# Comparisons for one-hots merged across tiles, buckets and units in the building stage of a graph network kernel

## The chip, the cores and the metric

The program runs on one core of a Trainium2 chip. The metric is the device time of one execution in microseconds, lower is better. The median of three executions stands for a kernel.

## The reference

The kernel computes two graph network layers over 12,500 nodes of 64 features and 412,500 edges `(src, dst)`, sorted by `dst`. Layer 0 is a hypergraph convolution, used twice, whose sums run over the edges in both directions; layer 1 makes a message for each edge from both its ends and a weight, sums it at the row, and feeds a node network.

```python
def _hypergraph_conv(x, node_idx, edge_idx, D_inv, B_inv, W, b):
    xt = x @ W
    e = B_inv[:, None] * segment_sum(xt[node_idx], edge_idx, num_segments=NUM_HYPEREDGES)
    out = D_inv[:, None] * segment_sum(e[edge_idx], node_idx, num_segments=NUM_NODES)
    return out + b
...
h = maximum(_layernorm(x), 0.0)
x = x + _L0_gnn_ref(h, edge_index, ...)
h = maximum(_layernorm(x), 0.0)
x = x + _L1_gnn_ref(h, src, dst, edge_weight1, ...)
```

The sums over edges of layer 0 are done as matrix products: the kernel first builds the adjacency as a matrix of small counts, block by block (how many edges go from node m to node d), and then multiplies with it. The stage that builds it is called the building here; the change lies in it alone.

## The kernel before

**Chunks, tiles, groups.** The building goes through the edges in 49 chunks (`NCH`), each for 256 destination nodes. A chunk holds 70 tiles (`TC`) of 128 edges, in 14 groups (`NGR`) of five (`GT`). 102 buckets (`KEYS`) take the edges of a chunk by the block of 128 nodes of their source (98 of them, and four for the diagonal). A loop iteration holds two turns; a turn does the 14 groups of one chunk and, beside them, the 50 units of the chunk before it. In the groups 2 to 13 stand 42 units, three or four to a group, and the last eight (`LATE`) come in groups 0 and 1 of the next turn.

**A group, over five engines.** POOL writes the one-hots `OH` of five tiles, 128 x 102 bf16 each (`onehots`, L662; it runs up to a turn ahead). PE turns them into running counts per bucket in the PSUM bank `R` (`ranks`, L777 to L785). ACT copies the last tile's counts to `cb` for the next group (`count`, L910) and widens `OH` to fp32 (`widen`, L916). DVE takes for each edge its rank, that is its slot in its bucket, into `rk` (`ranks`, L1018 to L1020), and writes one-hots of the slot (`places`): for the first three tiles (`AT`) as bf16 in `LB` (L1032), which ACT then multiplies with the two payloads `pl` into `LH` (`scaled`, L926, six copies a group); for the other two DVE makes the multiplied one-hot `LH` at once (L1038). PE multiplies `OHf` and `LH` into the bank `S` (`buckets`, L799), one group later, between the second and the third unit of a group. The width of a one-hot grows from 16 to 88 slots over the first seven groups, and again over the last seven.

**A unit.** The filled buckets are transposed (`turned`), and DVE copies them to `SBk`, `SBe` and `SBd` (`sorted_`). Unit 0 is the diagonal; each of the units 1 to 49 takes two buckets, an even one and an odd one. For it DVE compares a column of sources and one of destinations with a row of numbers (`unit`, in pairs of units). For the even bucket the source one-hot is in `OA`, for the odd one in `OB` with the value 256; both destination one-hots are in `OD` (L1089 to L1097). PE sums the two products into 256 columns of one of four PSUM banks, `bank(u)`, so that a sum is even count + 256 x odd count (`counts`, L825 and L826). ACT copies it to `RB` as int16, which is two bytes, each the fp8 code of a small count, and sums the row into `gs` (`keep`, L965):

```python
e.matmul(b[:, 0:256], lhsT=even, rhs=OD[k % PAIRS][:, y, :, 0], start=True, stop=False)
ins = e.matmul(b[:, 0:256], lhsT=odd, rhs=OD[k % PAIRS][:, y, :, 1], start=False, stop=True)
...
e.activation(RB[n % NSLOT][:, k, :].bitcast(i16), bank(u)[:, 0:256], ACT.Copy,
             accum_out=gs[:, u:u + 1]).then_inc(a_u, 1)
```

Three units later PE multiplies `RB` with the node features (`sums`, L841, four products). SP stores `RB`, in seven pieces of seven units, also transposed. Twice a turn DVE takes the row sums `gs` apart into their two bytes and keeps the greatest (`counted`, L1138 to L1145).

**What sets the order.** Each engine runs its list in the order in which the functions `step` and `turn` write it; semaphores hold it back. `past` and `wait_ge` are such waits. Rings of buffers bound the distance: two of `R`, `LB`, `LH` and `OHf`, five (`PAIRS`) of `OA`, `OB` and `OD`, four banks `PS`, four pieces of `RB`.

The stages after the building read the stored blocks, multiply with them, and do layer 1. Their lines are numbered from about 1215 on.

## Time and profile before

| | us |
|---|---|
| median of three executions | 8857.22 |
| lowest, highest | 8846.52, 8869.20 |
| the profiled execution | 8864.02 |
| its span, first to last instruction | 8862.3 |
| the building in it, from the page's slices | about 200 to 3340 |

The profile is of one execution. Its time and its span differ by 1.7 us, which lie around the instructions. Busy times of an engine count the time in which at least one of its instructions runs; consecutive instructions of DVE and ACT overlap by some 0.1 us, so durations of single ones add up to more than the busy time, and the distance from start to start tells what one costs in a row. A timeline row merges equal neighbours (x3) and gives the start of the first and the time to the end of the last.

### The profile page before, as it was taken

How to read it: one execution, taken by the hardware profiler on the slowest of the kernel's cores; microseconds unless marked ns; L12 is line 12 of the kernel's file. 1: busy time of each engine (PE TensorE's matmuls, PEld its weight loads, DVE VectorE, ACT ScalarE, POOL GpSimd, SP SyncE). 2: the span in 40 equal slices, each digit the busy share in tenths (PEclk: the TensorE clock that was granted, in tenths of full speed). 3: DMA queues.
4: the chain of work that ended last, by engine and by line, in shares of the span. 5: the costliest groups of instructions: out<-in, count | busy, mean ns of one | idle time of the engine just before them, and what ended most of it. 6: DMA issues, size and time to landing. Idle time of an engine off the chain costs nothing. (4 is left out here: it accounts for less than half of the span.)

```text
span 8862.3 us, 258190 instructions
## 1 busy us (share of the span) xinstructions
PE 7877.5 (89%) x80997; PEld 7191.2 (81%) x80997; DVE 7406.3 (84%) x20481; ACT 5157.5 (58%) x14322; POOL 2812.5 (32%) x4182
## 2 busy tenths in 40 slices
PE   2989998999989988999888899869999999999997
PEld 2777777777777778999788888759998999999995
DVE  7999999999999995777688888548888888888884
ACT  3777777777777770000577788425555555555553
POOL 4977778777777750000000000001111111111110
PEclk9999999999999999999799999759999999999998
DMA  2767667766676677666699999643333333333333
GB/s 71 158 152 157 154 153 157 155 155 153 156 156 153 156 159 199 190 191 170 148 223 222 214 245 245 139 142 109 104 106 106 103 106 106 105 104 105 107 104 74
DMA packets 1523049, 1310.03 MB, mean 148 GB/s; under 512 B 797344, under 2 KB 1337364, under 8 KB 1521212
## 3 DMA queue, kind: packets, MB, share of 16 engines
q1 hardware_dynamic: 1506126, 1269.86, 58.6%
q0 software_dynamic: 14112, 26.84, 1.2%
q8 instruction: 593, 9.72, 0.4%
q14 instruction: 378, 3.10, 0.1%
q10 hardware_dynamic: 1840, 0.53, 0.0%
HBM read 777.89 MB, written 361.62 MB: 129 GB/s over the span
## 5 line engine op out<-in xcount | busy, mean ns | idle before, releaser
L662 POOL TENSOR_SCALAR OH<-iot,kd 128x102 bf16<-128x102 bf16 x3440 | 2285.3, 683 | 3.5 <-PE S L799 3.5
L2257 POOL DMA_INDIRECT Qx<-tab_q,tidx x294 | 320.9, 1091 | 4904.5 <-DVE skt L2291 2584.5
L1478 PE MATMUL wp<-AF,XS 128*128 128x256 f32 x9604 | 1196.3, 283 | 167.6 <-issue 123.4
L841 PE MATMUL HP<-T3a,RB 128*128 128x193 bf16 x9604 | 1209.2, 249 | 124.3 <-ACT RB L965 124.3
L1478 PEld LDWEIGHTS wp<-AF,XS 128*128 128x128 f32 x9604 | 1148.5, 191 | 198.4 <-issue 198.3
L1504 ACT ACTIVATE AF<-RG 128x1536 fp32r<-128x1536 uint8 x686 | 1022.9, 1491 | 332.6 <-PE wp L1478 226.0
L965 ACT ACTIVATE RB<-PS 128x256 int16<-128x256 f32 x2401 | 895.6, 379 | 520.2 <-PE PS L826 479.2
L2278 ACT ACTIVATE Z<-Zb 128x512 f32<-128x512 f32 x882 | 556.1, 630 | 994.3 <-DVE Zb L2335 948.8
L841 PEld LDWEIGHTS HP<-T3a,RB 128*128 128x128 fp8e4 x9604 | 858.8, 98 | 249.1 <-issue 160.8
L926 ACT ACTIVATE LH<-LB,pl 128x64 f32<-128x64 bf16 (+8 forms) x4116 | 1008.4, 330 | 0.0
L2335 DVE TENSOR_TENSOR Zb<-p,eb2s 128x512 f32<-128x512 f32 x882 | 609.3, 691 | 450.1 <-PE p L2228 276.9
L2228 PEld LDWEIGHTS p<-eW2s,Y 128*128 128x128 f32 x7056 | 940.2, 194 | 31.8 <-issue 7.3
L2228 PE MATMUL p<-eW2s,Y 128*128 128x128 f32 x7056 | 947.7, 278 | 4.0 <-issue 3.8
L1558 DVE CAST AF<-RG 128x2048 fp32r<-128x2048 uint8 x686 | 812.3, 1222 | 148.7 <-PE wp L1478 55.0
L1097 DVE TENSOR_TENSOR OD<-iot,SBd 128x512 bf16<-128x512 bf16 x2401 | 932.6, 427 | 0.0
L799 PE MATMUL S<-LH,OHf 128*102 128x144 f32 (+9 forms) x6860 | 863.2, 274 | 14.4 <-ACT LH L926 11.8
L1343 PE MATMUL hp<-ACC,RG 128*128 128x193 bf16 x9604 | 822.1, 247 | 4.0 <-DMA RG<-adjT 4.0
L1343 PEld LDWEIGHTS hp<-ACC,RG 128*128 128x128 fp8e4 x9604 | 814.8, 98 | 7.9 <-issue 4.2
L799 PEld LDWEIGHTS S<-LH,OHf 128*102 128x102 f32 x6860 | 770.5, 172 | 42.4 <-issue 32.9
L825 PE MATMUL PS<-OD,OA 128*128 128x256 bf16 x2401 | 668.5, 279 | 150.3 <-DVE OD L1097 142.5
L2271 ACT ACTIVATE Y<-pT,eb1s 128x512 f32<-128x512 f32 x882 | 592.1, 671 | 221.1 <-remote 136.6
L2240 PE MATMUL pA<-Zp,Os 128*128 128x256 f32 x3528 | 649.7, 307 | 25.2 <-DVE Zp L2343 25.0
(344 smaller groups left out, 15460.4 us busy)
## 6 DMA issues: line engine op xcount, KB each, us to landing
RG<-adjT SPq DMA_DIRECT2D x1372, 224.0 KB, 6.6
sdb<-bk SPq DMA_DIRECT2D x245, 768.0 KB
adj<-RB SPq DMA_DIRECT2D x343, 448.0 KB, 2.8
adjT<-RT SPq DMA_DIRECT2D x686, 224.0 KB, 3.8
...
WR<-wk SPq DMA_DIRECT2D x882, 9.0 KB
...
```

Source lines behind the costliest of these rows:

```text
L662: ins = e.tensor_scalar(OH[:, g * GT + k, :], iot1[:, 0:KEYS], kd[:, g * GT + k:g * GT + k + 1], None, ALU.is_equal)
L799: ins = e.matmul(slots_to(g, w), lhsT=OHf[g % 2][:, k, :], rhs=LH[g % 2][:, k, :, 0:w], start=False, stop=True, skip_group_check=True)
L825: e.matmul(b[:, 0:256], lhsT=even, rhs=OD[k % PAIRS][:, y, :, 0], start=True, stop=False)
L841: ins = e.matmul(HP[:, h * W3:(h + 1) * W3], lhsT=pair[:, x_, h * P:(h + 1) * P], rhs=T3a[:, 2 * (u - 1) + x_, :], start=False, stop=True, ...
L926: ins = e.activation(LH[g % 2][:, k, c, 0:w], LB[g % 2][:, k, 0:w], ACT.Copy, scale=pl[:, c, t:t + 1])
L965: e.activation(RB[n % NSLOT][:, k, :].bitcast(i16), bank(u)[:, 0:256], ACT.Copy, accum_out=gs[:, u:u + 1]).then_inc(a_u, 1)
L1097: ins = e.tensor_tensor(OD[k % PAIRS][:, y, :, :], iot2[:, :, :], SBd[:, b + 2 * y:b + 2 * y + 2].unsqueeze(1).to_broadcast([P, 256, 2]), ...
L1343: ins = e.matmul(ps[b][:, h * W:(h + 1) * W], lhsT=piece(n, k_, h), rhs=tin3[:, n * 2 * PIECE + k_, 0:W], start=False, stop=True, skip_gro ...
L1478: ins = e.matmul(ps[b][:, 0:256], lhsT=XS[:, n * PB + m, :, :].rearrange("p c f -> p (c f)"), rhs=AF[:, (b + n) % 3, m, :], start=n == 0 a ...
L1504: e.activation(floats((b + n) % 3, VB, PB), counts(n, VB, PB), ACT.Copy).then_inc(h_ca, 1)
L1558: e.tensor_copy(floats((b + n) % 3, 0, VB), counts(n, 0, VB)).then_inc(h_cd, 1)
L2228: ins = e.matmul(p2[g % 2][:, t * P:(t + 1) * P], lhsT=Y[g % 2][:, t * P:(t + 1) * P], rhs=nW["eW2s"][:, :], start=True, stop=True)
```

## The change

Four things change, all in the building.

- **Slot one-hots.** DVE writes the bf16 one-hots `LB` of all five tiles with one comparison, as wide as the widest of the five, with fp32 inputs (`places`). ACT multiplies two tiles of a group (`AT` is 2) and DVE the other three, in one instruction, after the units of the group (`scaled`).
- **Source and destination one-hots.** One comparison writes `OA` for the four buckets of a pair of units, and one writes `OD` for both units. `OB` is gone.
- **Counts.** The products of the even and the odd bucket go to separate halves of the bank, 256 columns each, and ACT copies 512 values to bytes, reading the two halves in turn.
- **The check of row sums** needs no taking apart: one maximum instead of five instructions.

```diff
@@ -21,7 +21,7 @@
-AT = 3
+AT = 2
@@ -509,11 +507,11 @@
-OA = [sbt(p1, f"OA{n}", [P, 2 * P], bf16) for n in range(PAIRS)]
-OB = [sbt(p1, f"OB{n}", [P, 2, P], bf16) for n in range(PAIRS)]
+OA = [sbt(p1, f"OA{n}", [P, 4 * P], bf16) for n in range(PAIRS)]
 OD = [sbt(p1, f"OD{n}", [P, 2, 256, 2], bf16) for n in range(PAIRS)]
-SBe = sbt(p1, "SBe", [P, NCH], bf16)
+iot4 = sbt(p1, "iot4", [P, P, 4], bf16)
+SBs = sbt(p1, "SBs", [P, BLK], bf16)
@@ -591,9 +588,16 @@
-def by_rank(g, up, down, w):
-    return up[:, 0:w] if g < HG else down[:, P - w:P]
+def used(t):
+    w, g = wide_at(t), t // GT
+    a = 0 if g < HG else wide_at(g * GT + GT - 1) - w
+    return slice(a, a + w)
+def by_rank(g, n, w):
+    v = iofo[:, 0:w] if g < HG else iofr[:, P - w:P]
+    return v.unsqueeze(1).to_broadcast([P, n, w])
@@ -796,7 +800,7 @@
-                ins = e.matmul(slots_to(g, w), lhsT=OHf[g % 2][:, k, :], rhs=LH[g % 2][:, k, :, 0:w],
+                ins = e.matmul(slots_to(g, w), lhsT=OHf[g % 2][:, k, :], rhs=LH[g % 2][:, k, :, used(g * GT + k)],
@@ -820,10 +824,10 @@
-                even = OA[k % PAIRS][:, 0:n * P].rearrange("p (m y) -> p m y", y=n)[:, :, y]
-                odd = OB[k % PAIRS][:, y, :]
-                e.matmul(b[:, 0:256], lhsT=even, rhs=OD[k % PAIRS][:, y, :, 0], start=True, stop=False)
-                ins = e.matmul(b[:, 0:256], lhsT=odd, rhs=OD[k % PAIRS][:, y, :, 1], start=False, stop=True)
+                at = OA[k % PAIRS][:, 0:2 * n * P].rearrange("p (m y) -> p m y", y=2 * n)
+                e.matmul(b[:, 0:256], lhsT=at[:, :, 2 * y], rhs=OD[k % PAIRS][:, y, :, 0], start=True, stop=True)
+                ins = e.matmul(b[:, 256:512], lhsT=at[:, :, 2 * y + 1], rhs=OD[k % PAIRS][:, y, :, 1],
+                               start=False, stop=True, skip_group_check=True)
@@ -921,9 +925,9 @@
             past(e, p_s, i * NGR + (g - 1))
             for k in range(AT):
                 t = g * GT + k
-                w = wide_at(t)
+                w = used(t)
                 for c in range(2):
-                    ins = e.activation(LH[g % 2][:, k, c, 0:w], LB[g % 2][:, k, 0:w], ACT.Copy, scale=pl[:, c, t:t + 1])
+                    ins = e.activation(LH[g % 2][:, k, c, w], LB[g % 2][:, k, w], ACT.Copy, scale=pl[:, c, t:t + 1])
             ins.then_inc(a_lh, 1)
         def record(c):
@@ -962,8 +966,8 @@
-            e.activation(RB[n % NSLOT][:, k, :].bitcast(i16), bank(u)[:, 0:256], ACT.Copy,
-                         accum_out=gs[:, u:u + 1]).then_inc(a_u, 1)
+            e.activation(RB[n % NSLOT][:, k, :].bitcast(u8).rearrange("p (n x) -> p n x", x=2),
+                         bank(u)[:, :].rearrange("p (x n) -> p n x", x=2), ACT.Copy, accum_out=gs[:, u:u + 1]).then_inc(a_u, 1)
@@ -1018,27 +1022,25 @@
             e.tensor_reduce(rk[:, t:t + GM], R[g % 2][:, 0:GM * KEYS].rearrange("p (t k) -> p t k", k=KEYS), AX, ALU.max)
             t += GM
             e.tensor_tensor_reduce(out=rj[:, :], in0=R[g % 2][:, GM * KEYS:GT * KEYS], in1=OH[:, t, :],
-                                   scale=1.0, scalar=0.0, op0=ALU.mult, op1=ALU.add, accum_out=rk[:, t:t + 1]).then_inc(v_rk, 1)
-        def places(i, g, pl):
+                                   scale=1.0, scalar=float(OWN - 1), op0=ALU.mult, op1=ALU.add, accum_out=rk[:, t:t + 1]).then_inc(v_rk, 1)
+        def places(i, g):
             e.wait_ge(v_rk, i * NGR + (g + 1))
             if g == NGR - 1:
                 e.tensor_tensor(mxr[:, :], mxr[:, :], rk[:, :], ALU.max).then_inc(v_mx, 1)
             past(e, p_s, i * NGR + (g - 1))
             past(e, a_lh, i * NGR + (g - 1))
-            for k in range(AT):
-                t = g * GT + k
-                w = wide_at(t)
-                ins = e.tensor_scalar(LB[g % 2][:, k, 0:w], by_rank(g, iot1, iotr, w), float(OWN - 1), rk[:, t:t + 1], ALU.add, ALU.is_equal)
-            ins.then_inc(v_lb, 1)
-            for k in range(AT, GT):
-                t = g * GT + k
-                w = wide_at(t)
-                ranked = by_rank(g, iofo, iofr, w) if k < GM else by_rank(g, iot1, iotr, w)
-                ins = e.scalar_tensor_tensor(LH[g % 2][:, k, :, 0:w], ranked.unsqueeze(1).to_broadcast([P, 2, w]),
-                                             rk[:, t:t + 1], pl[:, :, t:t + 1].to_broadcast([P, 2, w]),
-                                             ALU.is_equal, ALU.mult)
-            ins.then_inc(v_lh, 1)
+            t, w = g * GT, wide_at(g * GT + GT - 1)
+            e.tensor_tensor(LB[g % 2][:, :, 0:w], by_rank(g, GT, w), rk[:, t:t + GT].unsqueeze(2).to_broadcast([P, GT, w]),
+                            ALU.is_equal).then_inc(v_lb, 1)
+        def scaled(i, g, pl):
+            e.wait_ge(v_lb, i * NGR + (g + 1))
+            n, t, w = GT - AT, g * GT, wide_at(g * GT + GT - 1)
+            e.tensor_tensor(LH[g % 2][:, AT:GT, :, 0:w], LB[g % 2][:, AT:GT, 0:w].unsqueeze(2).to_broadcast([P, n, 2, w]),
+                            pl[:, :, t + AT:t + GT].rearrange("p c t -> p t c").unsqueeze(3).to_broadcast([P, n, 2, w]),
+                            ALU.mult).then_inc(v_lh, 1)
         def filled(i):
@@ -1058,8 +1060,8 @@
-            e.tensor_copy(SBk[:, :], S[:, TR:TR + 2 * KEYS])
-            e.tensor_copy(SBe[:, :], S[:, TR:TR + BLK].rearrange("p (n x) -> p n x", x=2)[:, :, 0])
+            e.tensor_copy(SBk[:, :], S[:, TR + KEYS + BLK:TR + 2 * KEYS])
+            e.tensor_copy(SBs[:, :], S[:, TR:TR + BLK])
@@ -1078,25 +1080,18 @@
             if u == 0:
                 past(e, p_u, c * NU + (1 - NU))
                 for q in range(4):
-                    b = KEYS + BLK + q
-                    ins = e.tensor_scalar(OZ[:, q, :], iot1[:, :], SBk[:, b:b + 1], None, ALU.is_equal)
+                    ins = e.tensor_scalar(OZ[:, q, :], iot1[:, :], SBk[:, q:q + 1], None, ALU.is_equal)
                 ins.then_inc(v_un, 1)
             elif u % 2:
                 k = (u - 1) // 2
                 past(e, p_u, c * NU + (2 * k - 7 if k != 4 else 0))
-                for y in range(2 if u < NU - 1 else 1):
-                    b = 2 * (u + y - 1) + 1
-                    e.tensor_scalar(OB[k % PAIRS][:, y, :], iot1[:, 0:P], SBk[:, b:b + 1], 256.0, ALU.is_equal, ALU.mult)
+                n = 2 if u < NU - 1 else 1
                 b = 2 * (u - 1)
-                if u < NU - 1:
-                    e.tensor_tensor(OA[k % PAIRS][:, :].rearrange("p (m y) -> p m y", y=2), iot2[:, 0:P, :],
-                                    SBe[:, u - 1:u + 1].unsqueeze(1).to_broadcast([P, P, 2]), ALU.is_equal)
-                else:
-                    e.tensor_scalar(OA[k % PAIRS][:, 0:P], iot1[:, 0:P], SBk[:, b:b + 1], None, ALU.is_equal)
-                for y in range(2 if u < NU - 1 else 1):
-                    ins = e.tensor_tensor(OD[k % PAIRS][:, y, :, :], iot2[:, :, :],
-                                          SBd[:, b + 2 * y:b + 2 * y + 2].unsqueeze(1).to_broadcast([P, 256, 2]), ALU.is_equal)
-                ins.then_inc(v_un, 1)
+                e.tensor_tensor(OA[k % PAIRS][:, 0:2 * n * P].rearrange("p (m y) -> p m y", y=2 * n), (iot4 if n == 2 else iot2)[:, 0:P, :],
+                                SBs[:, b:b + 2 * n].unsqueeze(1).to_broadcast([P, P, 2 * n]), ALU.is_equal)
+                e.tensor_tensor(OD[k % PAIRS][:, 0:n, :, :], iot2[:, :, :].unsqueeze(1).to_broadcast([P, n, 256, 2]),
+                                SBd[:, b:b + 2 * n].rearrange("p (y x) -> p y x", x=2).unsqueeze(2).to_broadcast([P, n, 256, 2]),
+                                ALU.is_equal).then_inc(v_un, 1)
         def finish(c, n):
@@ -1132,17 +1127,9 @@
         def counted(c, h):
             a, b = (1, NU // 2) if h == 0 else (NU // 2, NU)
-            seen = c * 10 + (h * 5 + 1)
             e.wait_ge(a_u, c * NU + b)
-            e.wait_ge(v_gs, seen)
-            e.tensor_copy(gi[:, a:b], gs[:, a:b]).then_inc(v_gs, 1)
-            e.wait_ge(v_gs, seen + 1)
-            e.tensor_scalar(gl[:, 0, a:b], gi[:, a:b], 255, None, ALU.bitwise_and).then_inc(v_gs, 1)
-            e.tensor_scalar(gl[:, 1, a:b], gi[:, a:b], 8, None, ALU.arith_shift_right).then_inc(v_gs, 1)
-            e.wait_ge(v_gs, seen + 3)
-            e.tensor_tensor(mg[:, a:b], mg[:, a:b], gl[:, 0, a:b], ALU.max).then_inc(v_gs, 1)
-            e.wait_ge(v_gs, seen + 4)
-            e.tensor_tensor(mg[:, a:b], mg[:, a:b], gl[:, 1, a:b], ALU.max).then_inc(v_gs, 1)
+            e.wait_ge(v_gs, c * 2 + (h + 1))
+            e.tensor_tensor(mg[:, a:b], mg[:, a:b], gs[:, a:b], ALU.max).then_inc(v_gs, 1)
         def step(i, u, before):
             unit(i, u)
@@ -1171,11 +1158,13 @@
                 if rank:
                     if g == 0:
                         e.wait_ge(v_ld, i + 1)
-                    places(i, g, pl[b])
+                    places(i, g)
                 if unit_ and g == 2:
                     parts(i - 1)
                 for u in us[early:]:
                     step(k, u, before)
+                if rank:
+                    scaled(i, g, pl[b])
         e.wait_ge(c_init, 4)
         turn(0, 0, True, False, False, False)
```

DVE, near the end of a turn (group 12: a pair of units, then the places of the group, then the next pair). `c_pu`, `c_ps`, `c_alh`, `c_rk` and `c_vlb` are semaphores that PE's units, PE's buckets, ACT's copies, the ranks and the places raise. Before:

```order
L1089 TENSOR_SCALAR OB<-iot,SBk 128x128 [waits c_pu]
L1089 TENSOR_SCALAR OB<-iot,SBk 128x128
L1092 TENSOR_TENSOR OA<-iot,SBe 128x256
L1097 TENSOR_TENSOR OD<-iot,SBd 128x512 x2
L1032 TENSOR_SCALAR LB<-iotr,rk 128x72 [waits c_alh,c_ps,c_rk]
L1032 TENSOR_SCALAR LB<-iotr,rk 128x72 x2
L1038 SCALAR_TENSOR_TENSOR LH<-iofr,rk,pl 128x2x72
L1038 SCALAR_TENSOR_TENSOR LH<-iotr,rk,pl 128x2x80
```

and after:

```order
L1090 TENSOR_TENSOR OA<-iot,SBs 128x512 [waits c_pu]
L1092 TENSOR_TENSOR OD<-iot,SBd 128x1024
L1034 TENSOR_TENSOR LB<-iofr,rk 128x5x80 [waits c_alh,c_ps,c_rk]
L1041 TENSOR_TENSOR LH<-LB,pl 128x6x80 [waits c_vlb]
L129 REGISTER_ALU
L1090 TENSOR_TENSOR OA<-iot,SBs 128x512 [waits c_pu]
L1092 TENSOR_TENSOR OD<-iot,SBd 128x1024
```

Five instructions of the pair have become two, and five of the places have become two, the second of which waits for the first.

ACT, a group with four units (`c_pr`, `c_oh` and `c_pu` are raised by PE's ranks, POOL and PE's units). Before:

```order
L910 ACTIVATE cb<-R 128x102 [waits c_pr]
L916 ACTIVATE OHf<-OH 128x510 [waits c_ps,c_oh]
L948 REGISTER_ALU
L965 ACTIVATE RB,rows_of<-PS 128x256 [waits c_pu]
L948 REGISTER_ALU
L965 ACTIVATE RB,rows_of<-PS 128x256 [waits c_pu]
L948 REGISTER_ALU
L965 ACTIVATE RB,rows_of<-PS 128x256 [waits c_pu]
L948 REGISTER_ALU
L965 ACTIVATE RB,rows_of<-PS 128x256 [waits c_pu]
L926 ACTIVATE LH<-LB,pl 128x64 [waits c_ps,c_vlb]
L926 ACTIVATE LH<-LB,pl 128x64 x5
```

and after:

```order
L914 ACTIVATE cb<-R 128x102 [waits c_pr]
L920 ACTIVATE OHf<-OH 128x510 [waits c_ps,c_oh]
L952 REGISTER_ALU
L969 ACTIVATE RB,rows_of<-PS 128x512 [waits c_pu]
L952 REGISTER_ALU
L969 ACTIVATE RB,rows_of<-PS 128x512 [waits c_pu]
L952 REGISTER_ALU
L969 ACTIVATE RB,rows_of<-PS 128x512 [waits c_pu]
L952 REGISTER_ALU
L969 ACTIVATE RB,rows_of<-PS 128x512 [waits c_pu]
L930 ACTIVATE LH<-LB,pl 128x64 [waits c_ps,c_vlb]
L930 ACTIVATE LH<-LB,pl 128x64 x3
```

The order is the same; each unit's copy is twice as long in elements, and two of the six scaled copies are gone.

## Rows read from the trace of the kernel before

**Rows 1.** The profile page, its first section: busy time, share of the span, instructions.
```profile
PE 7877.5 (89%) x80997; PEld 7191.2 (81%) x80997; DVE 7406.3 (84%) x20481; ACT 5157.5 (58%) x14322; POOL 2812.5 (32%) x4182
```

**Rows 2.** Busy time of each engine in a stretch of the building: window, PE, PEld, DVE, ACT, POOL, PEclk, DMA share, GB/s.
```profile
1500.00:2500.00 1000.00, 906.61 (x8423) 762.74 (x8422) 965.03 (x4225) 768.69 (x3375) 778.28 (x1199) 0.98 0.70 154
```

**Rows 3.** Instructions of one line, the OD one-hots: duration ns min/median/max, first and last start.
```profile
L1097 DVE TENSOR_TENSOR OD<-iot,SBd x2401: 408/414/725, 200.0 to 3333.9; 128x512 bf16<-128x512 bf16 x185
```

**Rows 4.** Timeline of DVE, one group and its check of the counts: start us, us, what.
```profile
1526.52 0.62 DVE L1032 TENSOR_SCALAR LB<-iotr,rk 128x48 bf16<-128x48 bf16 x3
...
1527.67 0.51 DVE L1089 TENSOR_SCALAR OB<-iot,SBk 128x128 bf16<-128x128 bf16 x2
1528.10 0.28 DVE L1092 TENSOR_TENSOR OA<-iot,SBe 128x256 bf16<-128x256 bf16 x1
1528.31 0.75 DVE L1097 TENSOR_TENSOR OD<-iot,SBd 128x512 bf16<-128x512 bf16 x2
1528.98 0.24 DVE L1138 CAST gi_of<-rows_of 128x24 int32<-128x24 f32 x1
...
1529.54 0.21 DVE L1143 TENSOR_TENSOR mg<-mg,gl_of 128x24 f32<-128x24 f32 x1
1529.79 0.19 DVE L1145 TENSOR_TENSOR mg<-mg,gl_of 128x24 f32<-128x24 f32 x1
1529.95 0.58 DVE L1018 TENSOR_REDUCE rk<-R 128x4 f32<-128x408 f32 x1
```

**Rows 5.** Timeline of PE over the same time: start us, us, what [idle before <-releaser].
```profile
1524.49 0.29 PE L825 MATMUL PS<-OD,OA 128*128 128x256 bf16 x1 [0.78 <-DVE OD L1097]
...
1525.07 0.34 PE L777 MATMUL R<-OH,Uo 128*128 128x408 bf16 x1
...
1525.95 0.27 PE L825 MATMUL PS<-OD,OA 128*128 128x256 bf16 x1
...
1526.51 0.28 PE L825 MATMUL PS<-OD,OA 128*128 128x256 bf16 x1
...
1527.07 1.06 PE L799 MATMUL S<-LH,OHf 128*102 128x80 f32 x10
1527.97 0.28 PE L825 MATMUL PS<-OD,OA 128*128 128x256 bf16 x1
```

**Rows 6.** Timeline of PE, a group of wide tiles.
```profile
1509.53 1.47 PE L799 MATMUL S<-LH,OHf 128*102 128x144 f32 x10
1510.84 0.28 PE L825 MATMUL PS<-OD,OA 128*128 128x256 bf16 x1
```

**Rows 7.** Timeline of ACT over the same time.
```profile
1526.71 0.23 ACT L910 ACTIVATE cb<-R 128x102 bf16<-128x102 f32 x1
...
1527.36 0.37 ACT L965 ACTIVATE RB<-PS 128x256 int16<-128x256 f32 x1
...
1527.72 0.37 ACT L965 ACTIVATE RB<-PS 128x256 int16<-128x256 f32 x1
...
1528.85 1.47 ACT L926 ACTIVATE LH<-LB,pl 128x48 f32<-128x48 bf16 x6
1530.23 0.23 ACT L910 ACTIVATE cb<-R 128x102 bf16<-128x102 f32 x1
```

**Rows 8.** Instructions of single lines, durations: the nearest to the forms that are added.
```profile
L1107 DVE TENSOR_TENSOR et<-raw x49: 277/284/292, 267.7 to 3339.1; 128x128 f32<-128x128 f32 x49
...
L2335 DVE TENSOR_TENSOR Zb<-p,eb2s x882: 679/692/693, 5971.4 to 8694.4; 128x512 f32<-128x512 f32 x177
...
L2354 DVE TENSOR_REDUCE ao<-pA x49: 680/684/691, 6028.8 to 8698.3; 128x256 f32<-128x512 f32 x49
...
L971 ACT ACTIVATE raw<-HP x49: 484/484/493, 263.5 to 3338.5; 128x386 f32<-128x386 f32 x49
```

**Rows 9.** POOL in the stretch 1000 to 3000 us: its one-hots, and its wait.
```profile
L662 POOL TENSOR_SCALAR OH<-iot,kd x2166: 528/590/1077, 999.8 to 2999.6; 128x102 bf16<-128x102 bf16 x197
...
POOL kd L647 <- DMA ld<-pay: 443.5, 31, 15.5
```

More of the change, by code:

```diff
@@ L492, in gnn_kernel @@
                 gs = sbt(p1, "rows_of", [P, NU], fp32)
-                gi = sbt(p1, "gi_of", [P, NU], i32)
-                gl = sbt(p1, "gl_of", [P, 2, NU], i32)
                 mg = sbt(p1, "mg", [P, NU], fp32)
@@ L497, in gnn_kernel @@
                 LH = [sbt(p1, f"LH{n}", [P, GT, 2, P], fp32) for n in range(2)]
-                LB = [sbt(p1, f"LB{n}", [P, AT, P], bf16) for n in range(2)]
+                LB = [sbt(p1, f"LB{n}", [P, GT, P], bf16) for n in range(2)]
                 OHf = [sbt(p1, f"OHf{n}", [P, GT, KEYS], fp32) for n in range(2)]
@@ L530, in gnn_kernel @@
                 room = sbt(p1, "room", [P, KEYS], bf16)
-                iotr = sbt(p1, "iotr", [P, P], bf16)
                 iofr = sbt(p1, "iofr", [P, P], fp32)
                 d_ct = sem("c_dct")
-                SBk = sbt(p1, "SBk", [P, 2 * KEYS], fp32)
+                SBk = sbt(p1, "SBk", [P, 4], fp32)
                 Ui = sbt(p1, "Ui", [P, P], bf16)
@@ L609, in _ @@
                         for t in range(TC):
-                            e.memset(lim[:, t:t + 1], WIDE[t % HT] + 0.5 + (OWN - 1 if t % GT < GM else 0))
+                            e.memset(lim[:, t:t + 1], WIDE[t % HT] + OWN - 0.5)
                         e.memset(room[:, 0:BLK], float(SLH))
                         e.memset(room[:, BLK:KEYS], float(SLD))
-                        e.iota(iotr[:, :], pattern=[[-1, P]], base=P, channel_multiplier=0, allow_small_or_imprecise_dtypes=True)
+                        e.iota(iot4[:, :, :], pattern=[[1, P], [0, 4]], base=1, channel_multiplier=0, allow_small_or_imprecise_dtypes=True)
                         e.iota(iofr[:, :], pattern=[[-1, P]], base=OWN + P - 1, channel_multiplier=0, allow_small_or_imprecise_dtypes=True)
@@ L954, in keep @@
                             if u == 1:
-                                past(e, v_gs, c * 10 - 8)
+                                past(e, v_gs, c * 2)
                             if u == NU // 2:
-                                past(e, v_gs, c * 10 - 3)
+                                e.wait_ge(v_gs, c * 2 + 1)
                             if k == 0:
@@ L1193, in _ @@
                         counted(NCH - 1, 1)
-                        e.wait_ge(v_gs, 10 * NCH + 1)
+                        e.wait_ge(v_gs, 2 * NCH + 1)
                         e.wait_ge(d_ct, 16 * (NCH + 1))
```

## The prediction

> **What bounds the kernel now.** The page comes first: DVE and PE both look busy over the span, with POOL and ACT behind [rows 1]. That is an average over stages, and the change touches only the first long one, the building, so I read that stage alone. Its length comes from the OD one-hots: they run from 200.0 to 3333.9 us, 3134 us for 49 chunks, which makes 63.96 us for one turn of the loop [rows 3]. A stretch of 1000 us inside it gives the shares: DVE 96.5%, PE 90.7%, POOL 77.8%, ACT 76.9%, or 61.7, 58.0, 49.8 and 49.2 us of a turn. The TensorE clock is granted at 0.98, so almost always 2.4 GHz [rows 2]. The DVE timeline has no gap in which it waits for another engine: one instruction follows the other from the placing of a group to the next reduction [rows 4]. PE, however, stops before a unit's first product for 0.78 us, released by DVE's OD [rows 5]. So DVE ends the turn, and PE has some slack.
>
> How much is PE's own work? Its starts in a stretch where it waits for nothing give it: the ranks of a group 0.88 us (1525.07 to 1525.95), one unit with its sums 0.56 us (1525.95 to 1526.51), the buckets of a narrow group 0.90 us [rows 5], of a wide one 1.31 us [rows 6]. Per turn: 14 x 0.88 = 12.3, 49 x 0.56 = 27.4, 14 x about 1.1 = 15.4, and under 1 us of small ones: **55.5 us**. The 58.0 of the busy share counts tails that can overlap. The change leaves PE with the same number of products and columns, so this is the floor of the turn afterwards.
>
> **The change, part by part (per turn).**
> *Targets of two units.* On DVE a pair of units takes, start to start, from 1527.67 to 1528.98 = 1.31 us: two OB, one OA, two OD [rows 4]. The new pair is one OA of 512 elements and one OD of 1024, both 16-bit in all operands, as OD is now. A 512 form hands over after 0.75 - 0.41 = 0.34 us (the second OD starts this long after the first: the pair lasts 0.75, one lasts 0.414 [rows 3, 4]); from 256 elements (0.28 us) to 512 (0.414) it is 0.134 us more, so two times that for 1024: 0.34 + 0.27 = 0.61. New pair 0.95 us; with the hold-ups that lie in the 1.31 (undisturbed it would be near 1.20), I take 1.02. Saved 24 x 0.29 = 7.0 us; the odd last unit gains nearly nothing.
>
> *Slot one-hots.* Before, three LB and two LH for a group take 1526.52 to 1527.67 = 1.15 us [rows 4]. Now LB is one comparison of 5w elements, with fp32 inputs, and LH one product of 6w, issued after the group's units; nobody is late for it there, since PE's buckets of a group stand two units into the next one. No such form is in the trace; the nearest fp32 rows are 0.284 us for 128 and 0.692 for 512 elements, 1.06 ns per element [rows 8]. For w = 48: 240 elements 0.40 us, and because LH waits for LB's result where they are neighbours, another 0.04 us (a wait on its own result costs 1529.79 - 1529.54 - 0.21 [rows 4]); LH, 288 elements, 0.45 less the 0.08 by which the next one starts early: 0.37. Together 0.81 against 1.15. For w = 80 it is 0.57 + 0.54 = 1.11, about what stands there now, for 88 a loss. Over widths of 24 to 88 I take 0.1 us per group, 1.4 us; bounds 0 and 4.
>
> *Counts.* The check of the row sums (CAST to the second MAX) takes 1528.98 to 1529.95 = 0.97 us, twice a turn; one MAX stays, 0.25: saved 1.4 us. The copies behind the transpose save 0.1.
>
> DVE then: 61.7 - 7.0 - 1.4 - 1.4 - 0.1 = **51.8 us**.
>
> *ACT.* It loses a third of the scaled copies: 28 x 0.23 us (six take 1528.85 to 1530.23) = 6.4. It gains in every unit: even and odd counts now lie in 512 PSUM columns and not summed in 256. 256 take 0.37 us and hand over to the next unit after 0.36 [rows 7], 386 take 0.484 [rows 8], 0.8 to 0.9 ns per element, so 512 take about 0.59, 0.22 more: 49 x 0.22 = 10.8. ACT: 49.2 + 10.8 - 6.4 = **53.6 us**. The copy also reads PSUM in another order, one element from each half in turn, 1024 bytes apart. No ACT row shows that. One bound is no cost: DVE reads PSUM in pairs 512 bytes apart in its reduction of pA, 0.684 us for 512 elements, as fast as the neighbour that reads it in order, 0.692 [rows 8]. The other bound is half the speed, 0.43 us more a unit (one more 0.83 ns for each of 512). I take the first, since the row is a strided PSUM read of the same size. The Trainium skill, in "Advanced Engine Details and Errata", Memory Cachelines, says that PSUM has lines of 8 bytes and that access patterns whose neighbours are not contiguous slow matmuls significantly; it names matmuls, not ACT's reads. By that rule, carried over to ACT, the second bound would hold, and the sum would be that of the first rival.
>
> *PE.* The same two products per unit, into separate columns. The weights are now read from OA with three elements between neighbours (before one or none); a load is covered by the 256 columns before it. I cost it at nothing; if it lost 0.05 us uncovered on 98 loads, it would be 5 us. *POOL* fills another table before the loop and has the same work in it. Stages behind the building read the same bytes.
>
> **The sum.** PE needs 55.5 us, ACT 53.6, DVE 51.8 and POOL 49.8 (it waits 443.5 / 31 = 14.3 us of a turn for the next chunk's load [rows 9], which gives it room). PE becomes the bound, with ACT and DVE within 7%. A lone bound now reaches 96.5%; 55.5 / 0.965 = 57.5. Because ACT must follow each unit within four PSUM banks and is nearly as full, I add 0.3: **57.8 us**. That is 6.16 us less a turn, x 49 = 302 us. The profiled execution took 8864.0 us (span 8862.3), 7 above the median of 8857.2: the forecast is 8857 - 302 = 8555 us. What is late next is PE's own chain, in which no part of this change lies.
>
> **Rivals.**
> 1. *ACT reads the two halves at half speed (slower than before).* ACT would need 53.6 + 49 x 0.43 = 74.7 us, above the 64 of now, and the turn would follow it: about 75.5, + 11.5 x 49 = +560, **9420 us**. It decides from about 0.2 us more per unit than I take. Against it is the row of the pA reduction. Chance 0.08.
> 2. *DVE loses its two-elements-a-step rate in the new forms (slower).* The OD copy now repeats iot2 over a third dimension. At the fp32 rate of 1.06 ns, 1024 elements take 0.54 us more and 512 0.27: 24 x 0.81 = 19 us, DVE 71, turn 73.5, + 470, **9330 us**. Against it: OD already repeats its second operand. Chance 0.05.
> 3. *POOL becomes the bound.* Its one-hots take 0.528 us at best and 1.077 at worst [rows 9]. 70 of them at the best would be 37.0 us a turn, and POOL is busy for 49.8, so some 11 us are hold-ups beside DVE (a few other instructions are in the 12.8 between). Longer DVE instructions with no reduction between them could hold it longer: if the hold-ups doubled, POOL would need 61 and with its load the turn would be 62: - 96, **8760 us**. The Trainium skill, "SBUF — State Buffer", Who interferes with whom, says that a DVE instruction with two SBUF inputs and a GpSimd instruction that reads SBUF hold each other up, the later one for the whole of the other. The spread of 528 to 1077 ns agrees [rows 9]. Chance 0.10.
> 4. *Nothing to measure.* ACT's and PE's waits for each other swallow what DVE gives; turn 63.5 or more, **8840 us**. For it: PE already waits at times for ACT. Chance 0.04.
>
> **How the numbers follow.** My forecast has the remaining 0.73. Its own bounds: a turn of 55.8 (PE without a gap) gives 8457, one of 61.3 (three nearly full engines in line) gives 8727. With the start of rival 3 taken in, the range is **8450 to 8750**. A measurement of this kernel tells 0.3% (27 us) from nothing. Faster: 0.73 + 0.10 = 0.83; same 0.04; slower 0.08 + 0.05 = 0.13.
>
> **What would show it.** In the changed profile: OD of 1024 at 0.68 us and OA at 0.41; LB at 0.3 to 0.6; the copy of 512 at 0.59; the OD rows spanning 49 x 57.8 = 2830 us; DVE near 90% of the stage and PE at or above 96%; PE's wait for OD gone. A copy near 1.0 us, or an OD near 1.2, or POOL without its wait for the load would prove me wrong, each in the way of its rival.

## The result, and the profile after

The changed kernel took 8568.1 us (median of 4 runs, 8535.9 to 8580.4), the one before 8856.7 (4 runs, 8846.5 to 8869.2): ratio 0.9668, 95% interval 0.9639 to 0.9697. That is faster, by 289 us, and 13 us above the forecast. The profiled execution of the changed kernel took 8580.4 us, span 8578.6.

First the place of the gain. The rows are the weight load of the last products of the building (L853, before L849), the products of the next stage (L1332, before L1343) and those of the stage behind it (L1467, before L1478), each with its first and last start. Of before:

```profile
L849 PEld LDWEIGHTS HP<-TD,DG x98: 96/97/152, 263.0 to 3338.2; 128*128 128x128 bf16 x98
...
L1343 PE MATMUL hp<-ACC,RG x9604: 244/247/368, 3364.5 to 4198.6; 128*128 128x193 bf16 x196
...
L1478 PE MATMUL wp<-AF,XS x9604: 274/281/582, 4293.8 to 5656.6; 128*128 128x256 f32 x196
```

and of after:

```profile
L853 PEld LDWEIGHTS HP<-TD,DG x98: 95/97/118, 269.0 to 3029.8; 128*128 128x128 bf16 x98
...
L1332 PE MATMUL hp<-ACC,RG x9604: 244/247/368, 3059.5 to 3893.3; 128*128 128x193 bf16 x196
...
L1467 PE MATMUL wp<-AF,XS x9604: 276/281/582, 3988.9 to 5361.0; 128*128 128x256 f32 x196
```

The building ends 308 us earlier, the next stage starts 305 earlier. The wp stage then lasts 1372 us in place of 1363, and what follows it 3218 in place of 3206 (8862.3 - 5656.6, 8578.6 - 5361.0). So of 305 us gained, 284 reach the end of these two executions. The change has nothing in those stages; 21 us is 0.25% of the whole and less than the 44 us between the fastest and the slowest execution of the changed kernel, and I don't explain it.

Now the turn. The stretch of [rows 2] in the changed kernel:

```profile
1500.00:2500.00 1000.00, 962.40 (x9375) 858.96 (x9373) 921.96 (x2586) 913.99 (x3278) 989.80 (x1327) 1.00 0.80 173
```

And the instruction that opens POOL's turn, in the middle of the building, of before and of after:

```profile
L647 POOL TENSOR_TENSOR kd<-ld,ddc x37: 302/434/1367, 338.2 to 2665.4; 128x70 f32<-128x70 f32 x37
```

```profile
L651 POOL TENSOR_TENSOR kd<-ld,ddc x41: 302/303/810, 350.9 to 2671.9; 128x70 f32<-128x70 f32 x41
```

One turn is (2671.9 - 350.9) / 40 = **58.03 us**; before it was 2327.2 / 36 = 64.64. All turns below are worked out from this row of their kernel. Over all 49 chunks, by the OD rows as in [rows 3], it is (3023.4 - 200.8) / 49 = 57.60 in place of 63.96, so 311 us in all:

```profile
L1092 DVE TENSOR_TENSOR OD<-iot,SBd x1225: 410/689/831, 200.8 to 3023.4; 128x1024 bf16<-128x1024 bf16 x168, 128x512 bf16<-128x512 bf16 x7
```

But the engine that fills the turn is not the one I named. PE is busy for 96.2% (55.9 us a turn), ACT 91.4% (53.0), DVE 92.2% (53.5), and **POOL for 99.0%: 57.4 us**, against 50.3 before (77.8% of 64.64; the prediction's 49.8 takes the same share of 63.96). The group that answers to [rows 9], and the other POOL instructions that read SBUF in each turn, from 1000 to 2800 us (columns: shapes, count, busy us, mean ns, idle before); of before:

```profile
L662 POOL TENSOR_SCALAR OH<-iot,kd 128x102 bf16<-128x102 bf16 x1947 | 1299.7, 686 | 2.3 <-PE S L799 2.3
L670 POOL TENSOR_SCALAR DG<-idb,scc 128x128 bf16<-128x128 bf16 x56 | 39.7, 717 | 0.0
...
L647 POOL TENSOR_TENSOR kd<-ld,ddc 128x70 f32<-128x70 f32 x28 | 12.3, 441 | 400.9 <-DMA ld<-pay 400.9
```

of after:

```profile
L666 POOL TENSOR_SCALAR OH<-iot,kd 128x102 bf16<-128x102 bf16 x2173 | 1644.2, 775 | 0.0
L674 POOL TENSOR_SCALAR DG<-idb,scc 128x128 bf16<-128x128 bf16 x62 | 77.3, 1256 | 0.0
...
L651 POOL TENSOR_TENSOR kd<-ld,ddc 128x70 f32<-128x70 f32 x31 | 9.9, 319 | 11.0 <-POOL OH L666 11.0
```

The wait of 14.3 us a turn for the load is gone, and POOL's idle time is only its wait for its own results. The same one-hot, with no word of it changed, takes 775 ns in place of 686: 70 x 0.089 = 6.2 us a turn. DG takes 1256 in place of 717: 2 x 0.54 = 1.1. Together 7.3, which is all of the 7.1 us that POOL has gained. Where it goes shows in the two timelines. DVE after:

```profile
1748.22 0.75 DVE L1092 TENSOR_TENSOR OD<-iot,SBd 128x1024 bf16<-128x1024 bf16 x1
1748.89 0.17 DVE L1132 TENSOR_TENSOR mg<-mg,rows_of 128x24 f32<-128x24 f32 x1
1749.42 0.58 DVE L1022 TENSOR_REDUCE rk<-R 128x4 f32<-128x408 f32 x1 [0.36 <-ACT cb L914]
1749.92 0.26 DVE L1024 CUSTOM_DVE_ANT_0 rj<-R,OH 128x102 f32<-128x102 f32 x1
...
1750.10 0.42 DVE L1090 TENSOR_TENSOR OA<-iot,SBs 128x512 bf16<-128x512 bf16 x1
1750.44 0.68 DVE L1092 TENSOR_TENSOR OD<-iot,SBd 128x1024 bf16<-128x1024 bf16 x1
1751.04 0.60 DVE L1034 TENSOR_TENSOR LB<-iofr,rk 128x360 bf16<-128x360 f32 x1
```

POOL's three one-hots of the last two microseconds (ns, min/median/max):

```profile
L666 POOL TENSOR_SCALAR OH<-iot,kd x3: 530/615/1052, 1749.9 to 1751.4; 128x102 bf16<-128x102 bf16 x3
```

The one at 1749.9 starts beside the reduction and the short custom instruction and takes 530, although OA starts 0.2 us into it. The one of 1052 ns starts at 1750.39, while OA runs and just before OD starts. So an identical instruction takes 0.53 us or about twice that, by when it meets DVE's instructions. Over the whole program the one-hot's median is 772 ns and its maximum 1891, in place of 589 and 1441.

Who waits, and for what (us in total, times, longest), from 1000 to 2800 us:

```profile
ACT scc L955 <- POOL TD L676: 63.9, 30, 3.3
...
PE HP L853 <- POOL TD L676: 44.0, 30, 2.7
```

PE's wait for OD, 142.5 us in 220 times over the program before, has shrunk to 3.6 us in 3. In its place PE and ACT each wait once a turn for POOL's TD. So the profile speaks for POOL as the bound; PE at 96.2% is near enough that it had to be tested.

### The profile page after: what moved, and what is told of

Its sections match the earlier page's. It is cut to its first block and busy times, and to the rows that moved or that the text cites. A ratio compares the mean times of both kernels' runs of the same rounds, so it can differ in the third digit from the quotient of the medians.

```text
span 8578.6 us, 250515 instructions
## 1 busy us (share of the span) xinstructions
PE 7767.5 (91%) x80997; PEld 7231.2 (84%) x80997; DVE 6974.8 (81%) x14454; ACT 5320.2 (62%) x12950; POOL 3168.3 (37%) x4182
## 5 line engine op out<-in xcount | busy, mean ns | idle before, releaser
L666 POOL TENSOR_SCALAR OH<-iot,kd 128x102 bf16<-128x102 bf16 x3440 | 2586.5, 770 | 0.0
L969 ACT ACTIVATE RB<-PS 128x512 uint8<-128x512 f32 x2401 | 1407.6, 598 | 112.8 <-PE PS L829 68.1
L1467 PE MATMUL wp<-AF,XS 128*128 128x256 f32 x9604 | 1205.9, 284 | 167.1 <-issue 113.7
L1467 PEld LDWEIGHTS wp<-AF,XS 128*128 128x128 f32 x9604 | 1154.6, 191 | 201.4 <-issue 200.7
L845 PE MATMUL HP<-T3a,RB 128*128 128x193 bf16 x9604 | 1187.3, 246 | 40.9 <-ACT RB L969 40.8
L1092 DVE TENSOR_TENSOR OD<-iot,SBd 128x1024 bf16<-128x1024 bf16 x1225 | 854.6, 698 | 0.0
L803 PE MATMUL S<-LH,OHf 128*102 128x144 f32 (+9 forms) x6860 | 846.0, 271 | 0.3 <-ACT LH L930 0.3
L1332 PE MATMUL hp<-ACC,RG 128*128 128x193 bf16 x9604 | 822.9, 247 | 2.8 <-DMA RG<-adjT 2.8
L1332 PEld LDWEIGHTS hp<-ACC,RG 128*128 128x128 fp8e4 x9604 | 815.5, 98 | 6.9 <-issue 3.1
L930 ACT ACTIVATE LH<-LB,pl 128x16 f32<-128x16 bf16 (+7 forms) x2744 | 696.7, 335 | 0.0
```

Of the source, the lines that this page charges most:

```text
L666: ins = e.tensor_scalar(OH[:, g * GT + k, :], iot1[:, 0:KEYS], kd[:, g * GT + k:g * GT + k + 1], None, ALU.is_equal)
L803: ins = e.matmul(slots_to(g, w), lhsT=OHf[g % 2][:, k, :], rhs=LH[g % 2][:, k, :, used(g * GT + k)], start=False, stop=True, skip_group_ch ...
L845: ins = e.matmul(HP[:, h * W3:(h + 1) * W3], lhsT=pair[:, x_, h * P:(h + 1) * P], rhs=T3a[:, 2 * (u - 1) + x_, :], start=False, stop=True, ...
L930: ins = e.activation(LH[g % 2][:, k, c, w], LB[g % 2][:, k, w], ACT.Copy, scale=pl[:, c, t:t + 1])
L969: e.activation(RB[n % NSLOT][:, k, :].bitcast(u8).rearrange("p (n x) -> p n x", x=2), bank(u)[:, :].rearrange("p (x n) -> p n x", x=2), AC ...
L1092: e.tensor_tensor(OD[k % PAIRS][:, 0:n, :, :], iot2[:, :, :].unsqueeze(1).to_broadcast([P, n, 256, 2]), SBd[:, b:b + 2 * n].rearrange("p ( ...
```

## The experiments

Each kernel starts from the changed one unless its text says otherwise. The kernel before took between 8677 and 8857 us on the chips used. The changed kernel took 8568 us on one of them and 8389 on another with the same turn, 58.03 and 58.06 (e5; the last section has the stage that differs). So ratios to the kernel before are compared, and turns. The runs without a ratio are single executions. "One-hot" is the mean of POOL's OH from 1000 to 2800 us, and the shares are those of the stretch 1500 to 2500.

| kernel | ratio to before [95%] | turn us | PE | DVE | ACT | POOL % | one-hot ns |
|---|---|---|---|---|---|---|---|
| before | 1 | 64.64 | 90.7 | 96.5 | 76.9 | 77.8 | 686 |
| changed | 0.9668 [0.9639, 0.9697] | 58.03 | 96.2 | 92.2 | 91.4 | 99.0 | 775 |
| changed, other chip (e5) | 0.9663 [0.9628, 0.9698] | 58.06 | 96.1 | 92.3 | 91.5 | 99.0 | 776 |
| e1, diagonal on DVE | 0.9562 [0.9529, 0.9594] | 56.47 | 98.6 | 95.1 | 94.0 | 99.0 | 802 |
| e1 again | 0.9565 [0.9544, 0.9586] | 56.41 | 98.6 | 95.1 | 94.0 | 99.0 | 801 |
| e2, units alone | 0.9850 [0.9814, 0.9885] | 61.32 | 95.1 | 88.7 | 95.5 | 89.1 | 754 |
| e3, slots alone | 0.9921 [0.9895, 0.9947] | 63.24 | 91.2 | 97.0 | 69.4 | 81.0 | 700 |
| e4, OD in two | 0.9616 [0.9583, 0.9648] | 57.31 | 97.4 | 96.4 | 92.3 | 95.6 | 741 |
| e6, half the sums | 0.9711 [0.9676, 0.9747] | 58.42 | 88.9 | 91.4 | 90.3 | 99.0 | 795 |
| e7, ACT in order | one execution, 8386 us | 58.07 | 96.3 | 92.1 | 91.4 | 99.0 | 777 |
| e8, e1 with OD in two | 0.9637 [0.9589, 0.9685] | 57.40 | 97.1 | 96.5 | 92.0 | 89.7 | 742 |
| e9, e1 with a table | 0.9561 [0.9535, 0.9586] | 56.44 | 98.6 | 95.2 | 93.8 | 98.4 | 803 |
| e10, e1 with half the sums | one execution, 8525 us | 57.56 | 89.7 | 92.0 | 90.5 | 94.3 | 779 |
| e11, a dose on POOL | 0.9729 [0.9702, 0.9756] | 59.21 | 95.0 | 90.1 | 89.7 | 99.0 | 771 |

**e1: POOL gives the diagonal to DVE.** The four instructions of `diagonal` go from POOL's turn to DVE, into group 7.

```diff
@@ POOL, turn
                                 onehots(i, g)
-                                if behind and g == NGR // 2:
-                                    diagonal(i - 2)
@@ DVE, turn
+                                if unit_ and g == NGR // 2:
+                                    diagonal(i - 1)
```

> The changed kernel, but the four small operations of the diagonal (DG twice, selfc, TD) are DVE's and no longer POOL's; the same work otherwise. In the changed kernel POOL is busy for 98.98% of a turn of 58.04 us and PE for 96.2%. POOL theory: POOL bounds the turn, PE and ACT wait for its TD. Then POOL loses about 3.2 us a turn (DG 2 x 1.2 with its hold-ups, TD 0.5, selfc 0.2), the turn falls to 55.5 to 56.3 us, and the time by 85 to 125 us, to 8445 to 8485. PE theory (that of the prediction): PE bounds the turn, POOL only happens to be full; the turn stays at 57.7 to 58.4, or grows a little by DVE's 0.7 us, and the time stays within 20 us of 8568.

The turn fell by 1.6 us, to just above the range of the POOL theory, and the kernel is 1.0% faster than the changed one (0.9562 against 0.9663, from two chips). PE's products are the same and DVE has more to do, and both became fuller, as did ACT; so none of them had set the 58.03. POOL is at 99.0% again:

```profile
1500.00:2500.00 1000.00, 985.66 (x9653) 882.81 (x9651) 951.31 (x2738) 939.69 (x3370) 990.11 (x1295) 1.00 0.81 177
```

```profile
L666 POOL TENSOR_SCALAR OH<-iot,kd 128x102 bf16<-128x102 bf16 x2235 | 1749.5, 802 | 0.0
```

POOL got rid of about 3.3 us (DG 2.5, TD 0.5, selfc 0.26, by its rows of after), but its one-hots grew from 775 to 802 ns, which takes 70 x 0.027 = 1.9 back. Its copy `pl` came down from 663 to 336 ns, 0.3 more. What is left, 1.7, is about what the turn fell by. **e1 again** repeated it on another chip:

> e1 again as the base for the two beside it: ratio to before 0.956, turn 56.4 to 56.5 us.

The ratio is 0.9565 and the turn 56.41. This is the fastest version found (e9 equals it), faster than both kernels.

**e2 and e3: the parts alone.** e2 keeps the new targets and counts and brings the slot one-hots of before back (`AT = 3`, three LB and two LH a group). e3 is the kernel before with the new slot one-hots only.

```diff
@@ e2, DVE places
-                            e.tensor_tensor(LB[g % 2][:, :, 0:w], by_rank(g, GT, w), ...
+                            for k in range(AT):
+                                ins = e.tensor_scalar(LB[g % 2][:, k, 0:w], by_rank(g, iot1, iotr, w), ...
@@ e3, DVE places, against the kernel before
-                            for k in range(AT):
...
-                                ins = e.tensor_scalar(LB[g % 2][:, k, 0:w], by_rank(g, iot1, iotr, w), ...
...
+                            e.tensor_tensor(LB[g % 2][:, :, 0:w], by_rank(g, GT, w), ...
```

> The changed kernel with the slot one-hots of before: three LB and two LH instructions a group, ACT scales three tiles. Even and odd counts apart, one comparison for four buckets, one for two units, stay. By the terms of the prediction ACT needs 53.0 (measured) + 28 x 0.23 = 59.5 us a turn and becomes the bound: turn 60.5 to 62, time 8568 + 49 x (2.5 to 4) = 8690 to 8765. POOL theory: the same end, but if DVE's many short instructions let POOL in sooner, its one-hots go from 0.77 back towards 0.69 us and POOL falls under 55 us. If ACT hides it, the turn stays at 58 and the time at 8570.

> The kernel before with only the slot one-hots changed (LB of five tiles in one comparison, LH of three tiles in one product, ACT scales two tiles). By the prediction's term DVE saves 1.4 us of 61.7 (bounds 0 and 4): turn 63.0, bounds 60.4 and 64.4, time 8857 - 70, 8660 to 8857. If the gain of the whole change were mostly here, 8700 or less.

e3 is 1.4 us a turn below before, the size of the term in my sum. e2 is 3.3 us below, at 61.3, within what was expected. Together they would give 4.7, and the whole change gives 6.6. The row of e2 gives the likely reason:

```profile
1500.00:2500.00 1000.00, 951.20 (x8854) 819.75 (x8853) 887.12 (x3129) 955.32 (x3548) 891.20 (x1248) 0.99 0.76 162
```

ACT is the fullest there, at 95.5%: the copies of 512 have come and the two scaled copies a group have not gone. PE, at 95.1%, waits for ACT's results for 72.2 us between 1000 and 2800 (42.0 for RB and 30.2 for LH), where in the changed kernel it waits for 25.1. The new slot one-hots, worth 1.4 us by DVE's time, are worth 3.3 on top of e2; the reading is that they take work from ACT, and no run relieved ACT alone to show it. The one-hot of POOL rises by 14 ns from the slots alone and by 68 from the units alone.

**e4: OD by two instructions of 512 again.**

```diff
-                                e.tensor_tensor(OD[k % PAIRS][:, 0:n, :, :], iot2[:, :, :].unsqueeze(1)...
+                                for y in range(n):
+                                    ins = e.tensor_tensor(OD[k % PAIRS][:, y, :, :], iot2[:, :, :], ...
```

> The changed kernel with OD of a pair written by two instructions of 512 elements, as before, and not by one of 1024. DVE needs 24 x 0.06 = 1.5 us more a turn. PE theory: DVE is not the bound, so nothing: 8555 to 8585. POOL theory: if a long DVE instruction holds POOL up for its length, the split lets POOL in between, its one-hots fall from 0.77 to 0.73 us or less, POOL saves 2 to 4 us a turn and the time falls by 50 to 120. If the hold-up depends on DVE's total only, no change.

```profile
1500.00:2500.00 1000.00, 974.35 (x9486) 869.84 (x9486) 963.81 (x3028) 922.75 (x3312) 956.06 (x1342) 1.00 0.79 175
...
POOL kd L651 <- DMA ld<-pay: 79.6, 31, 4.6
```

More instructions on DVE, and a shorter turn by 0.75 us: 24 more of them a turn bring POOL's one-hot from 776 to 741 ns and POOL from 57.4 to 54.8 us, so it waits for the load again. DVE is then as full as in the kernel before, at 96.4%. Merging two OD into one, which was to save time, cost it here; the change as a whole pays. The relief is at the low end of what was expected (2.6 us of POOL's turn, the one-hot at 741 ns and not at 730), and the gain of some 40 us is below the 50 to 120 put down. With PE at 97.4% beside it, this run alone doesn't tell whether DVE ends the turn now. The difference in ratio to the changed kernel (0.9616 against 0.9668 and 0.9663) is near what the intervals can tell, and the turn, which repeats within 0.06 us between executions of one kernel, is the firmer sign.

**e5: the changed kernel once more**, on the chip of e6:

> The changed kernel as it is, for the runs beside it: the times of before moved between chips (8857 and 8688 us). With the ratio of 0.967 it takes 0.967 x before here; turn 58.0 us, POOL busy for 99% of it, as in its first profile.

The turn is 58.06, POOL at 99.0% and the one-hot 776 ns. So the turn is a property of the kernel, and e6 can be read against it.

**e6: PE relieved.** Two of the four HP products of a unit are left out, and so half of the sums; by the prices of the prediction this takes 8 us of PE's work out of a turn.

```diff
-                            for x_ in range(2):
+                            for x_ in range(1):
```

> The changed kernel without the products of the odd buckets in the sums (two of four products of each unit are left out, so the first convolution adds only half of its rows). PE loses 98 x 0.082 = 8.0 us a turn of its 55.5, and no other engine's work changes. PE theory (the prediction's): PE bounds the turn, which falls from 58.0 by 3 to 5 us, until DVE and ACT bound it: 150 to 250 us less than the changed kernel. POOL theory: the turn stays at 57.5 to 58.2 with POOL at 99%, and the time within 25 us of the changed kernel.

```profile
1500.00:2500.00 1000.00, 889.39 (x7673) 735.26 (x7672) 913.51 (x2574) 902.62 (x3266) 990.32 (x1315) 0.96 0.78 171
```

PE lost 4 us of busy time a turn (55.8 to 52.0; the granted clock fell from 1.00 to 0.96 in the stretch, so its products took longer), and the turn did not fall: 58.42 against 58.06. POOL stayed at 99.0%, without a wait for the load, and PE now waits for POOL's one-hots, 44.9 us in 11 times between 1000 and 2800, up to 4.2 at once. That fits a turn that POOL ends. But as a test of PE the run is weak: with its pauses and the lower clock, PE's chain alone may need some 57.6 us (e10), so no more than 0.5 us could have shown. The rise of 0.4 is a little outside the range for the POOL theory, and the time, 8431 us, is 41 above e5's, where 25 had been put down. The one-hots, at 795 ns, add 70 x 0.019 = 1.3 us, and the two DG, at 747 ns in place of 1292, give 1.1 of it back; why the hold-ups move so, I can't say.

**e7: ACT reads PSUM in order.** The copy of a unit reads and writes its 512 elements in their own order, so that the two halves are not interleaved in its output; this measures the disputed pattern.

```diff
-                            e.activation(RB[n % NSLOT][:, k, :].bitcast(u8).rearrange("p (n x) -> p n x", x=2),
-                                         bank(u)[:, :].rearrange("p (x n) -> p n x", x=2), ...
+                            e.activation(RB[n % NSLOT][:, k, :].bitcast(u8), bank(u)[:, :], ...
```

> The changed kernel, but ACT reads the 512 columns of a unit in their order and not one of each half in turn (so the counts stand in another order, and the convolutions use wrong pairs). If the strided read costs, the copy falls from 0.597 us; at half speed the strided one would have shown 1.0, so the most that can be found is what lies over 0.47 + 0.0. If PSUM is read at one element a step whatever the distance, 0.59 to 0.60 as before and the turn is the same within 0.3 us.

e5, with the pattern of the change, and then e7, in order:

```profile
L969 ACT ACTIVATE RB<-PS x2401: 577/597/745, 203.0 to 3029.0; 128x512 uint8<-128x512 f32 x185
```

```profile
L969 ACT ACTIVATE RB<-PS x2401: 577/597/741, 203.4 to 3027.7; 128x512 uint8<-128x512 f32 x185
```

The turn is 58.07. The pattern cost nothing. The Trainium skill, "Advanced Engine Details and Errata", Memory Cachelines, says that PSUM patterns whose neighbours are not contiguous slow matmuls. For ACT's reads a carried-over rule would be wrong; of matmuls these runs say nothing.

**e8: e1 and e4 together.**

> The diagonal on DVE (e1) and OD in two instructions (e4) together. e1 ended at 56.4 us a turn with POOL at 99.0% and PE at 98.6%; e4's split freed POOL of 2.7 us. If POOL still holds e1, PE's 55.6 is reached: turn 55.6 to 56.0, 20 to 40 us less than e1 in relation to before (ratio 0.952 to 0.954). If DVE, now at 95% of 56.4 = 53.7 and with 1.5 more, becomes as full as PE, the turn stays at 56.4 or rises to 57, ratio 0.956 to 0.960.

POOL has room now (89.7%, and it waits 180.1 us in 31 times for the load), but the turn is 57.40, as in e4 and above e1: DVE has the diagonal and 24 instructions more, and is at 96.5%. The two cures don't add up. PE is at 97.1%, below the 98.6% that it reaches in e1, so DVE is the likelier bound; no run relieved it there to show that. Read the other way, the merged OD that cost 0.75 us with the diagonal on POOL saves 0.9 with the diagonal on DVE (57.40 against 56.47).

**e9 and e10: what holds e1?** In e1 PE is at 98.6% and POOL at 99.0%. e9 puts the offsets `ddc` into a table before the loop, so that POOL loses one instruction a turn and a wait for its result:

```diff
-                            e.tensor_scalar(ddc[:, :], ddc[:, :], 256.0, None, ALU.add).then_inc(v_key, 1)
+                                            ddc[:, DS(i * 2, 2)].unsqueeze(2)...
```

> e1 (diagonal on DVE), and POOL no longer adds 256 to its offsets ddc in every turn: they stand in a table that it fills once. POOL loses one more instruction and a wait, 0.5 to 0.7 us a turn. e1 stood at 56.47 us a turn with POOL at 99.0% and PE at 98.6% (55.6 us). If POOL bounds e1: 55.8 to 56.0 us a turn, 20 to 35 us less time than e1, ratio to before 0.952 to 0.954. If PE bounds e1: 56.4 to 56.5, ratio 0.956.

e10 is e1 with the edit of e6 (half of the sums left out):

> e1 with half of the sums left out (as in e6: the first convolution adds only half of its rows), which takes 8.0 us a turn from PE. If PE bounds e1, the turn falls below 56.0 to POOL's or DVE's next bound (DVE at 95% of 56.4). If POOL bounds e1, it stays at 56.3 to 56.6, or rises where PE's pauses lower its granted clock, as in e6 (0.96, turn 59.7).

Neither tells. In e9 the turn stayed (56.44), but POOL was not relieved. The `ddc` instruction that went had taken 12.6 us in e1 between 1000 and 2800, and POOL's waits for its own results grew by 11.0, from 17.6 (11.2 and 6.4) to 28.6:

```profile
POOL kd L650 <- POOL OH L664: 15.2, 32, 0.5
...
POOL pl L658 <- POOL kd L650: 13.4, 32, 0.4
```

In e10 the turn rose to 57.56 with the clock at 0.96 in place of 1.00. POOL is at 94.3% there and waits for the load again, so it does not end that turn:

```profile
POOL kd L651 <- DMA ld<-pay: 97.2, 23, 11.8
```

(The text above puts e6's turn at 59.7; by the `kd` rows it is 58.42.) So whether POOL or PE ends e1's turn stays open.

**e11: a dose on POOL.** Eight fills a turn of a tile that nobody reads, one behind each of the groups 1 to 8.

```diff
                                 onehots(i, g)
+                                if 1 <= g <= 8:
+                                    e.iota(scrap[:, g - 1, :], pattern=[[1, P]], ...)
```

> The changed kernel with eight more instructions a turn on POOL, which nobody reads and nobody waits for: the filling of a scrap tile of 128 x 128 fp32 with numbers, 0.25 us each in the trace (2.0 us a turn, or 1.6 if neighbours overlap), one behind each of the groups 1 to 8. If POOL bounds the changed kernel (99.0% of 58.04 us), the turn grows by about the whole dose: 59.5 to 60.1 us, the time by 70 to 100 us (ratio to before 0.974 to 0.978). If POOL is full only because its one-hots wait where there is time, and PE bounds it, the one-hots take less (under 0.775 us on average) and the turn stays below 58.5.

```profile
L685 POOL IOTA scrap<- x392: 229/233/280, 153.5 to 3000.5; 128x128 f32 x196
...
ACT scc L958 <- POOL TD L677: 83.5, 30, 3.2
...
PE HP L856 <- POOL TD L677: 63.7, 30, 2.6
```

The dose is 8 x 0.233 = 1.86 us and the turn rose by 1.18 (1.14 against e5). That is outside the range in which POOL would take it one for one, and far from nothing. Of the other 0.7, most came back from the one-hots (771 in place of 775 ns, 0.3 us a turn) and from DG (1120 in place of 1256, 0.3 us), with DVE down from 92.2 to 90.1%; that a less dense DVE holds POOL up less is a reading of this one run. PE and ACT wait longer for TD, 2.1 and 2.8 us a turn in place of 1.5 and 2.1. And the fills themselves, which write SBUF and read nothing there, were never held up: 229 to 280 ns among 392, beside a DVE with which the one-hots take 527 to 1445 in the same trace.

Taken together: with PE's products unchanged, relief of POOL shortens the turn, whether by less work (e1) or by fewer hold-ups (e4), a load on POOL lengthens it (e11), and in the changed kernel POOL waits for nothing but its own results. POOL bounds the changed kernel. What POOL needs depends on DVE's instructions, so it is an elastic bound. That OD's length is one cause of the hold-ups is shown by e4, for 35 of the 89 ns; which of the other new forms makes the rest is not.

## Why the prediction was right, and where not

- **The number** (8555, range 8450 to 8750): measured 8568. The turn of 57.8 was measured as 57.60 by the OD rows and 58.03 in the middle; the 2830 us that these rows should span are 2823.
- **DVE's terms** held. OD of 1024 has a median of 0.689 us, OA of 512 0.418, LB 0.27 to 0.70 with medians of 0.467 and 0.451. A pair of units takes 1750.10 to 1751.04 = 0.94 us, elsewhere 1.05 (I took 1.02). DVE is busy for 53.5 us a turn, where the sum said 51.8. Of the 1.7, 0.7 is the reckoning (the sum started from 96.5% of 63.96 and not of 64.64), and LH is some 0.6: its mean for 288 elements is 0.495 us where I took 0.45, and for 480 it is 0.666 where I took 0.62 (0.54 and the overlap of 0.08; the fp32 rows give 0.66, so that was a slip in the sum), 14 times a turn. The rest is not traced. The slots' 1.4 us showed up alone in e3.
- **ACT's term** held: the copy takes 0.597 us (0.59), ACT 53.0 us (53.6). Rival 1 is refuted by e7, rival 2 by the rows of OD and OA.
- **PE's sum** held: 55.5 us, measured 55.9, at 96.2%, and its wait for OD is gone. But "PE becomes the bound" is the conclusion that failed: with the same products the turn is 57.31 in e4 and 56.47 in e1, where PE is at 98.6%. So the step from 55.5 to 57.8 failed too. It took 3.5% of idle time from DVE, the lone bound before, and added 0.3; PE alone needs 56.5 or less.
- **The step that failed** is "POOL fills another table before the loop and has the same work in it", with its 49.8 us carried over. It has the same instructions and needs 57.4 us, since 70 x (775 - 686) = 6.2 and two DG of 0.54 more went into hold-ups. The traces of before had the spread: I wrote down 528 at best and 1077 at worst, and gave it to rival 3 with 0.10. Its mechanism is what happened, and so is its sign, "POOL without its wait for the load". Its size wasn't: hold-ups were to double, from 11 to some 22 us, and they became 70 x (0.775 - 0.528) = 17, with the load's wait vanishing in place of adding to the turn.
- So the number was right by luck: POOL's needs happened to grow to 58.0, where I had put PE's too high at 57.8. Had PE been the bound, as in the forecast, the ratio of e1 (0.9562) says that about 8469 us would have been measured, still in the range but 86 below the forecast.
- The Trainium skill, "SBUF — State Buffer", Who interferes with whom, says that a DVE instruction with two SBUF inputs contends with a GpSimd one that reads SBUF and not with one that only writes. Both halves agree with e11's trace: one-hots 527 to 1445 ns, fills 229 to 280. That the later one waits for the whole of the other, as the prediction has it, is not settled by a trace here: the one-hot of 1052 ns above lost 0.52 us, beside an OA of 0.42 and an OD of 0.68.
